# Decoder block with routed experts: where VectorE and ScalarE fetch the expert number, and where ScalarE rounds the gate weights

## The reference

```
E, K, H = (8, 2, 352)
logits = x @ gate_w
scores = softmax(logits)
topk_w, topk_idx = top_k(scores, K)
g = silu(einsum('td,edh->teh', x, w_gate)) * einsum('td,edh->teh', x, w_up)
routed = einsum('teh,ehd,te->td', g, w_down, comb)
shared = silu(x @ sw_gate) * (x @ sw_up) @ sw_down
out = routed + shared
```

## Time and profile before

| | us |
|---|---|
| median of three runs | 1105.0 |
| lowest and highest | 1102.69, 1107.13 |
| the profiled execution | 1105.46 |
| its span, first to last instruction | 1103.7 |
| stage of the experts | from about 754 to 1077 of the span |

### The profile page before, as it was taken

The page is one execution under the profiler, slowest core; times in us unless marked ns, Lnnn a source line. Parts: engine busy times, 40 slices in busy tenths (PEclk is TensorE's granted clock), DMA queues, the critical chain, the costliest instruction groups (busy, mean ns, idle before and its releaser), DMA issues. The chain is left out here.

```text
span 1103.7 us, 17998 instructions
## 1 busy us (share of the span) xinstructions
PE 958.9 (87%) x5111; PEld 712.2 (65%) x5111; DVE 756.6 (69%) x1313; ACT 608.9 (55%) x918; POOL 463.0 (42%) x423
## 2 busy tenths in 40 slices
PE   5999999699999999945999999982879999999960
PEld 4556787344444444324889898872868888888850
DVE  3323655777777777418888888843867889888844
ACT  3433211477676776724444444432766888888844
POOL 2000000265555655656565656523233545555423
PEclk9999999799999999966999999995998999999985
DMA  7454700543342442033111111134794434444338
GB/s 249 153 191 161 238 22 1 115 115 90 82 114 66 105 99 73 1 101 114 56 51 58 58 57 57 49 108 146 251 283 78 70 69 74 76 70 73 68 46 306
DMA packets 80881, 115.71 MB, mean 105 GB/s; under 512 B 15680, under 2 KB 37056, under 8 KB 80832
## 3 DMA queue, kind: packets, MB, share of 16 engines
q1 hardware_dynamic: 66320, 90.69, 27.6%
q0 software_dynamic: 9760, 20.49, 10.1%
q10 hardware_dynamic: 4752, 3.94, 1.2%
HBM read 74.77 MB, written 40.31 MB: 104 GB/s over the span
## 5 line engine op out<-in xcount | busy, mean ns | idle before, releaser
L1759 DVE TENSOR_TENSOR we_lo<-w_all,we_hi 128x1408 fp32r<-128x1408 f32 (+1 forms) x117 | 189.1, 1666 | 31.4 <-ACT we_hi L1692 22.3
L612 POOL TENSOR_TENSOR pair_sum<-probs 128x2048 f32<-128x2048 f32 x32 | 146.4, 4575 | 96.6 <-ACT probs L756 96.6
L784 DVE TENSOR_REDUCE maxima<-ps_s 128x8 f32<-128x512 f32 x240 | 150.7, 685 | 51.9 <-PE ps_s L640 51.1
L1692 ACT ACTIVATE we_hi<-w_all 128x1408 fp32r (+1 forms) x117 | 161.5, 1413 | 37.3 <-PE e_ps_y L1818 19.8
L756 ACT ACTIVATE probs<-ps_st 128x512 f32<-128x512 f32 x256 | 143.1, 597 | 69.3 <-PE ps_st L695 65.6
L1663 POOL DMA_INDIRECT x_dram<-e_y,who x39 | 63.6, 1632 | 136.0 <-ACT e_y L1709 120.3
L1657 POOL DMA_INDIRECT xg<-x_dram,who x39 | 74.2, 1902 | 41.7 <-DMA who<-table_dram 24.6
L1448 PE MATMUL ps_gu<-sw_hi,x2T_hi 128*128 128x352 f32 (+1 forms) x256 | 88.2, 345 | 1.9 <-issue 1.5
L1448 PE MATMUL ps_gu<-sw_hi,x2T_lo 128*128 128x352 f32 (+1 forms) x256 | 84.1, 328 | 0.0
L1448 PE MATMUL ps_gu<-sw_lo,x2T_hi 128*128 128x352 f32 (+1 forms) x256 | 83.9, 328 | 0.0
L598 POOL MEMSET ones_sum<- 128x32 f32 x1 | 0.1, 125 | 186.8 <-POOLq L52 186.8
(11 more groups left out here) (251 smaller groups left out, 2493.0 us busy)
## 6 DMA issues: line engine op xcount, KB each, us to landing
qk_dram<-qk_ctx SPq DMA_DIRECT2D x32, 512.0 KB, 2.8
q_more<-qk_dram SPq DMA_DIRECT2D x60, 128.0 KB, 3.0
k_more<-qk_dram SPq DMA_DIRECT2D x60, 128.0 KB, 3.2
w_all<-in_L_ffn_w_gate_dram SPq DMA_DIRECT2D x8, 704.0 KB
w_all<-in_L_ffn_w_up_dram SPq DMA_DIRECT2D x8, 704.0 KB
q_first<-qk_dram SPq DMA_DIRECT2D x36, 128.0 KB, 3.0
k_first<-qk_dram SPq DMA_DIRECT2D x36, 128.0 KB, 3.2
x_dram<-x SPq DMA_DIRECT2D x16, 256.0 KB, 2.0
```

Source lines behind the costliest of these rows:

```text
L612: pool.tensor_tensor(pair_sum[:, h], probs[:, 2 * h], probs[:, 2 * h + 1], ALU.add).then_inc(added, 1)
L784: dve.tensor_reduce(by_tile[:, t, j, 1:9], bank(p, x).rearrange("p (g n) -> p g n", n=S // 8), axis=AX.X, op=ALU.max).then_inc(s_reduced, 1)
L1692: act.activation(w_hi[kind][:], raw(base, kind), ACT.Copy).then_inc(s[kinds[kind] + "_hi"], 1)
L1759: dve.tensor_tensor(w_lo[kind][:], raw(base, kind), w_hi[kind][:].bitcast(F32), ALU.subtract).then_inc(s[kinds[kind] + "_lo"], 1)
```

## The change

The number of the expert is no longer fetched inside `w_low` and `w_high`'s callers, but handed to them. VectorE fetches the number of tile j + 1 between `g_low(j - 1)` and `x_low(j + 1)`, and uses it after `multiply(j)` for the gate correction. ScalarE fetches it between `x_high(j + 1)` and `silu(j)`; the gate weights of tile j + 1 are then rounded ahead of `y_store(j - 2)` and the up weights behind it. The other fetches keep their places, and no instruction is added or taken away.

```
 def one(j, r):                                   # ScalarE
     p = r % 2
     if at(j, 1):
-        down_high(j - 1)
+        down_high(j - 1, expert_base(act, j - 1))
     if not is_last(j):
         x_high(j + 1, 1 - p)
+        base = expert_base(act, j + 1)
     silu(j, p)
     if at(j, 1):
         g_high(j - 1, 1 - p)
+    if not is_last(j):
+        gate_high(j + 1, base)
     if at(j, 2):
         y_store(j - 2, p)
     if not is_last(j):
-        hidden_high(j + 1)
+        up_high(j + 1, base)
...
 def one(j, r):                                   # VectorE
     p = r % 2
-    w_low(j, UP)
+    w_low(j, UP, expert_base(dve, j))
     if at(j, 1):
-        w_low(j - 1, DOWN)
+        w_low(j - 1, DOWN, expert_base(dve, j - 1))
         g_low(j - 1, 1 - p)
     if not is_last(j):
+        base = expert_base(dve, j + 1)
         x_low(j + 1, 1 - p)
     multiply(j, p)
     if not is_last(j):
-        w_low(j + 1, GATE)
+        w_low(j + 1, GATE, base)
```

More of the change, by code:

```diff
@@ L1710, in y_store, with down_high, gate_high, up_high @@
                                    scale=who[:, bass.ds(j, 1), 1].bitcast(F32)).then_inc(s["y_out"], 1)
-                def down_high(j):
-                    base = expert_base(act, j)
+                def down_high(j, base):
                     need(act, s["y_done"], j)
                     w_high(base, DOWN)
-                def hidden_high(j):
-                    base = expert_base(act, j)
+                def gate_high(j, base):
                     need(act, s["g_done"], j)
                     w_high(base, GATE)
+                def up_high(j, base):
                     need(act, s["u_done"], j)
@@ L1735, in one @@
                     if not is_last(j):
-                        hidden_high(j + 1)
-                hidden_high(0)
+                        up_high(j + 1, base)
+                base = expert_base(act, 0)
+                gate_high(0, base)
+                up_high(0, base)
                 x_high(0, 0)
@@ L1741, in _ @@
                 tiles(act, one)
-                down_high(NJ - 1)
+                down_high(NJ - 1, expert_base(act, NJ - 1))
                 g_high(NJ - 1, 0)
@@ L1755, in _, with w_low @@
             def _(dve):
-                def w_low(j, kind):
-                    base = expert_base(dve, j)
+                def w_low(j, kind, base):
                     dve.wait_ge(s[kinds[kind] + "_hi"], j + 1)
@@ L1784, in one @@
                     if not is_last(j):
-                        w_low(j + 1, GATE)
+                        w_low(j + 1, GATE, base)
                 dve.wait_ge(s["padded"], 1)
-                w_low(0, GATE)
+                w_low(0, GATE, expert_base(dve, 0))
                 x_low(0, 0)
                 tiles(dve, one)
-                w_low(NJ - 1, DOWN)
+                w_low(NJ - 1, DOWN, expert_base(dve, NJ - 1))
                 g_low(NJ - 1, 0)
```

## The result

| | before | changed |
|---|---|---|
| median, us (7 and 8 runs) | 1105.0 | 1093.71 |
| the profiled execution, us | 1105.46 | 1091.40 |
| its span, us | 1103.7 | 1089.7 |
| first `e_g` of the stretch, tile 7 | 835.8 | 832.7 |
| last `e_g`, tile 38 | 1060.8 | 1046.0 |

A forecast was written before the change was run, and what follows sets the result against it. Bound: a ring between PE and VectorE, 7.23 us a turn, from tile 7 to 38. 24 x 0.29 = 7.0 and 7 x 0.41 = 2.9 make 9.9 us, giving 1095.5 us; range 1088 to 1103, the forecast's own 1092 to 1099.

The forecast's parts named there:

- VectorE's ring decides: Expert stage, tiles 7 to 38: VectorE rather than PE decides when `e_g` starts; turns 6.8 to 7.05 us, chance 0.68.
- Fetch taken from behind `e_g`, minus 0.57: VectorE: the gate correction follows `e_g` back to back, at 0.44 us instead of 1.01, saving 0.57 us a tile.
- Fetch ahead of `xgT_lo`, `xgT_lo` 0.97 behind `e_gT_lo`: VectorE: the fetch counts in full there, `xgT_lo` at 0.97 us instead of 0.47; plus 0.21 us a tile.
- the first rival: VectorE's new fetch is free, done under the down correction; PE becomes the bound, 6.69 us a turn, 1087.8 us; chance 0.10.
- The rule weighed: Skill page: the sequencer fetches on while an instruction awaits semaphores; the prediction said the trace, load at 908.62, disagrees.
- Ring of the down weights, 6.94: Second ring through PE, ScalarE's down-weight rounding and VectorE: two turns in 13.87 us, 6.94 each, taken as the turn.
- Behind a jump 7.02: Seven of 31 turns follow a loop jump: 7.02 us instead of about 7.43, minus 0.41 each.
- ScalarE's new order worth nothing: ScalarE: gate weights ahead of `e_y` are insurance, worth nothing in the sum; the fetch ahead of silu costs nothing.
- Gathers hidden with 1.3 us to spare: GpSimd: `e_y`, scatter and gather come 1.3 us later, but gathers still land about 1.3 us before PE's transposes.
- Nothing lost at the end: Behind tile 38's `e_g` (last down weights, scatter, normalization): nothing gained, the end as before.
- Slower rival: VectorE's new fetch meets GpSimd's gather and takes 0.9 us: turn 7.54, 8.7 us lost, 1114 us; chance 0.09.
- The second rival: Gain given back by ScalarE's weights 0.3 us late or fetches of 0.5: 7.12 a turn, 1101 us; chance 0.13.

The follow-up runs named there:

- The double load: Changed kernel with the expert-number load done twice on VectorE, ahead of `xgT_lo`: ratio 1.0058 to the kernel before, turn 7.44 us.
- the two passes: Changed kernel with one of three down-product passes left out on PE: ratio 0.9905 to the kernel before, turn 6.87 us, 6.84 without the first.
- the fetch moved on: Changed kernel with VectorE's fetch one place earlier, between the down correction and `e_gT_lo`: 1089.94 us, ratio 0.9875 to the kernel before, turn 6.76 us.
- VectorE's part alone: Kernel before with only VectorE's fetch moved, ScalarE's lines as before: ratio 0.9908 to the kernel before, turn 6.91 us.
- ScalarE's part alone: Kernel before with only ScalarE's new order, VectorE fetching right ahead of each correction as before: ratio 0.9995, turn 7.26 us.

## Why the prediction was right, step by step

**VectorE's ring decides: right.** The double load, the two passes and the fetch moved on show it from three sides. But it isn't a ring of VectorE's work alone. The fetch starts when ScalarE's `e_gT_hi` is done, and that hangs on PE's `e_ps_g` and so on the gate correction; this is ScalarE's row in the turn shown above, ahead of the load at 900.14:

```profile
899.53 0.49 ACT L1704 ACTIVATE e_gT_hi<-e_ps_gT 128x384 fp32r<-128x384 f32 x1
```

The forecast turn was 6.94 with 7.02 behind a jump; it is 6.88, and no longer behind a jump than elsewhere. That is the 1.8 us between 9.9 and 11.7.

**Fetch taken from behind `e_g`, minus 0.57: right**, 1.01 to 0.42 or 0.43.

**Fetch ahead of `xgT_lo`, `xgT_lo` 0.97 behind `e_gT_lo`: the mis-sized term.** It is 0.90 when `e_gT_lo` starts as soon as `e_gT_hi` is there and down to 0.69 the longer the down correction still runs by then; 0.79 on average in the first profile. The sequencer goes on as soon as `e_gT_hi` is there: the load starts 0.12 to 0.14 us behind its end in every turn of the loop, and `xgT_lo` 0.92 to 0.96 behind it. In the turn shown the load starts at 900.14, ahead of `e_gT_lo`, which starts at 900.22. So a part of the fetch was hidden after all, and the first rival's mechanism was partly at work. I had used only the turn in which the sequencer stood at an unmet wait, though the prediction itself said that `e_gT_lo` is often ready when the down correction ends.

**The rule weighed.** The page "Perfetto Trace Analysis" of the Trainium skill, section "DVE / Act Engine Instruction", lets the sequencer go on while an instruction waits for its semaphores. The rows show both halves: at an unmet wait the load came only when `e_g` had started (908.52 and 908.62 in the earlier trace rows); with the wait met and only the datapath busy it came ahead. `e_g` alone wouldn't tell, since one of its two waits is an instruction of its own on the sequencer; `e_gT_lo` has a single wait, and there too the load never came before `e_gT_hi` was done. By the rule in full the turn would have been that of PE, 6.76; the changed kernel had 6.88.

**Ring of the down weights, 6.94: there, but not the bound.** The down correction waits for ScalarE in every turn, 0.20 to 0.22 us in the rows above. With the shorter fetch this ring too is shorter. The two-pass kernel, in which that wait is gone, has turns of 6.84, so the wait costs the changed kernel 0.07 us a turn at the most. To take 6.94 in place of VectorE's own 6.87 made the forecast too small; the 6.87 met the measured 6.88 partly by luck, since it has 0.97 for a fetch of 0.79 and no wait of the down correction.

**Behind a jump 7.02: too careful.** Of the two bounds given (no loss, or 0.3) the first held, as the load behind the jump takes 0.30 and not 0.89.

**ScalarE's new order worth nothing: right here**, by VectorE's part alone against the whole. It would be wrong of the faster kernel.

**Gathers hidden with 1.3 us to spare: wrong, at little cost.** PE's weight loads for the transposes wait for a gather 14 times, 6.1 us in all. By its own signs the prediction would have been wrong here ("if PE's matmuls wait for a gather"), and with the down correction (0.22 us where it allowed 0.2) it was at its limit. Neither costs much: 0.02 to 0.05 us a turn for the gathers, and 0.07 at the most for the down correction. This is from the waits of the changed kernel:

```profile
DVE we_lo L1763 <- ACT we_hi L1692: 6.3, 31, 0.3
PEld e_ps_xT L1816 <- DMA xg<-x_dram,who: 6.1, 14, 0.6
```

I had taken the scatter ahead of the gather at its old 1.6 us. It takes 2.9 now, and that ate the margin.

**Nothing lost at the end: off by 0.8 us.** The last four scatters of the changed kernel follow one another, each waiting for the one before it to land, as its chain of waits has it. Most scatters of the loop do that already, and start 0.80 us behind the landing of the one before.

```profile
1040.20 5.75 DMA x_dram<-e_y,who
...
1046.70 4.81 DMA x_dram<-e_y,who
...
1052.57 4.89 DMA x_dram<-e_y,who
...
1058.21 4.88 DMA x_dram<-e_y,who
```

**Slower rival: did not come**, but not for the reason given. The gather was to start 2.0 us behind the gate correction and be 2.9 us old at the fetch. It starts 3.4 us behind it (898.50 and 895.11), as the scatter ahead of it is longer, and is 1.5 to 1.9 us old at the fetch; about half of the gathers still run then. All loads on VectorE are at 0.30 to 0.32 even so. The rival missed by little: loads that started up to 1.0 us behind a gather were long (last section).

**Two slips in the sums.** With 9.9 us off, the median of 1105.0 gives 1095.1, not 1095.5. The second rival's 7.12 isn't what its terms give: 13.87 + 0.3 + 0.2 over two turns is 7.19, so about 2 us gained and not 4. Both are small.

## What to carry to other kernels

A fetch into a register isn't free because it is a "sequencer instruction": it holds everything behind it on its engine. Here it cost 0.57 us a turn behind `e_g`, 0.3 behind `e_gT_lo`, and nothing under the down correction, which is longer than the fetch and whose successor's wait is already met. So put it directly behind the longest instruction, not merely earlier. When a wait listed for a semaphore stands where a fetch does too, move the producer in an experiment before believing the name; here that changed only the label. And after each such step look for the next ring of nearly the same length: PE 6.76, `e_g` to `e_ps_g` and back 6.66, and GpSimd's scatter and gather near 6.7 stood close behind one another, so that each further step gave a tenth of a microsecond.

## What the runs showed of the hardware

**GpSimd's indirect DMAs take longer when they start under one of VectorE's corrections, while the corrections keep their length.** The scatter takes 1.59 us in the kernel before, and 2.9 in the changed one; the landings there are 5.7 to 6.4 us after the issue, and 4.5 to 5.1 with VectorE's part alone. The rows are of L1663 in 834 to 1040, first of the changed kernel, then with VectorE's part alone:

```profile
L1663 POOL DMA_INDIRECT x_dram<-e_y,who x30: 2561/2878/2957, 833.3 to 1033.6; - x30
```

```profile
L1663 POOL DMA_INDIRECT x_dram<-e_y,who x30: 1567/1594/1613, 838.3 to 1038.9; - x30
```

What tells them apart is what VectorE does as the scatter starts. In the changed kernel it starts at 895.48, 0.37 us behind a gate correction (895.11), which reads two operands from SBUF:

```profile
895.48 2.72 POOL L1663 DMA_INDIRECT x_dram<-e_y,who  x1 [1.38 <-ACT e_y L1709]
898.50 0.98 POOL L1657 DMA_INDIRECT xg<-x_dram,who  x1 [0.30 <-issue]
```

With VectorE's part alone `e_y` comes earlier and the scatter starts ahead of the correction. With ScalarE's part alone `e_y` is as late as in the changed kernel, but the correction is late too, and starts at 933.83, behind the scatter:

```profile
933.57 1.59 POOL L1663 DMA_INDIRECT x_dram<-e_y,who  x1 [2.98 <-ACT e_y L1709]
```

So it is neither the place of `e_y` nor the overlap as such, but which of the two starts first. The Trainium skill, "SBUF — State Buffer", section "Who interferes with whom", says that a VectorE instruction with two SBUF inputs contends with a GpSimd instruction that reads SBUF, and that the one issued first has the port until it ends while the other blocks. For GpSimd that fits. For VectorE it doesn't: corrections of 1408 columns take 1.61 to 1.65 us when a scatter or a gather is already running too, like the 1.63 us of the one at 936.48 in VectorE's part alone, which starts under a scatter (935.25 to 936.84). That the port is the cause wasn't tested by itself.

The fourteen profiles, read from 835 to 1040, give the size. All 144 scatters that start with no correction running take 1.57 to 1.61 us. The 270 that start under one take 1.43 to 1.52 us plus what is left of it: 2.72 for 1.25 left in the row above. Gathers do the same, which the two lengths of a gather in these kernels come from: 0.98 to 1.00 us with no correction running (93 of them), and 0.85 to 0.90 plus what is left for the 251 that start 0.06 us or more behind a correction's start, as in the earlier trace rows (2.13 us at 909.88, with 1.27 left). The 29 gathers that start within 0.04 us of a correction's start take 0.97 to 0.99 us in spite of it, like the one at 898.50 above.

**The load of a register has two lengths on VectorE.** In the kernel before, loads that started 0.3 us behind a gather took 0.9 us, the others mostly 0.3. In the changed kernel none is above 0.32 us, and with the fetch one place earlier they reach 0.92 again. Over the fourteen profiles, from 830 to 1045, 133 of 1285 loads take more than 0.4 us, and 128 of these start 0.05 to 1.0 us behind the start of a gather; only four loads that start in that range are short. What the load waits for there is left open, and so are the other five long ones.
